# Attention in a three-layer kernel: the third bank of transposed scores is written later and alternates with the third score bank of the unit ahead

## The reference

```python
Q = x @ W_Q.T; K = x @ W_K.T; V = x @ W_V.T          # 16 heads of 8 features
attn = jnp.einsum('bhqd,bhkd->bhqk', Q, K) * scale
attn = jnp.where(causal, attn, -inf)
probs = jax.nn.softmax(attn, axis=-1)
y = jnp.einsum('bhqk,bhkd->bhqd', probs, V)
return y.transpose(0, 2, 1, 3).reshape(Bx, Sx, Dm) @ W_O.T
```

## Time and profile before

| | |
|---|---|
| median of 3 runs | 1352.4 us (1349.47 to 1357.5) |
| profiled execution | 1349.75 us, span 1348.0 us |
| TensorE (PE) busy, whole span | 1238.0 us (92%), 11940 products |
| VectorE busy | 1107.1 us (82%) |
| ScalarE busy | 833.5 us (62%) |
| GpSimd busy | 554.5 us (41%) |
| attention's turns, 430 to 958 us | PE 482.57, DVE 427.02, ACT 361.95, POOL 173.56 us busy; mean granted clock 0.97 |

### The profile page before, as it was taken

One profiled execution on the slowest core, in us unless ns is written; L12 is line 12 of the kernel. 1 busy time (PEld: TensorE's weight loads), 2 busy tenths in 40 slices (PEclk: granted clock), 3 DMA queues, 4 the chain that ended last, 5 costly groups with the idle time before them and its releaser, 6 DMA issues. The chain is left out here.

```text
span 1348.0 us, 34907 instructions
## 1 busy us (share of the span) xinstructions
PE 1238.0 (92%) x11940; PEld 691.8 (51%) x11940; DVE 1107.1 (82%) x2686; ACT 833.5 (62%) x1477; POOL 554.5 (41%) x658
## 2 busy tenths in 40 slices
PE   5999999999979999999999999899899999999998
PEld 2555555555533555555555555555455555555554
DVE  6888888888975688888888888888688898988876
ACT  5665565656543566666666666666565656566564
POOL 3454544544530233333333333333354554554444
PEclk9999999999995799999999999999899999999999
DMA  6000000000000000000000000000000000000000
GB/s 186 2 1 1 0 0 0 0 0 0 1 1 1 1 1 2 2 2 2 2 2 2 1 2 2 1 2 2 2 2 16 9 16 8 16 8 16 8 9 25
DMA packets 21417, 11.85 MB, mean 9 GB/s; under 512 B 960, under 2 KB 21312, under 8 KB 21312
## 3 DMA queue, kind: packets, MB, share of 16 engines
q1 hardware_dynamic: 21312, 10.43, 2.8%
HBM read 6.23 MB, written 4.19 MB: 8 GB/s over the span
## 5 line engine op out<-in xcount | busy, mean ns | idle before, releaser
L672 POOL TENSOR_TENSOR h_lo<-h,h_hi 128x512 f16<-128x512 f32 x288 | 337.7, 1173 | 386.3 <-ACT h_hi L634 375.6
L1109 DVE TENSOR_REDUCE neg_max_at<-score_at 128x2 f16<-128x512 f32 (+1 forms) x384 | 254.4, 692 | 78.1 <-PE score_at L940 72.5
L1229 POOL TENSOR_SCALAR_AFFINE_SELECT probs_at<-probs_at 128x512 f32<-128x512 f32 x256 | 157.0, 637 | 352.4 <-ACT probs_at L1187 351.9
L634 ACT ACTIVATE h_hi<-h 128x512 f16<-128x512 f32 x288 | 180.6, 627 | 152.7 <-DVE h L435 150.8
L1187 ACT ACTIVATE probs_at<-prob_at 128x512 f32<-128x512 f32 x384 | 201.6, 598 | 79.3 <-PE prob_at L972 77.4
L435 DVE TENSOR_TENSOR h<-prod,gate_b 128x512 f32<-128x512 f32 x256 | 174.9, 683 | 53.9 <-PE gate_b L543 53.7
L564 PE MATMUL y_b<-w_hi,h_hi 128*128 128x128 f16 x1152 | 207.8, 219 | 2.6 <-POOL h_lo L672 2.6
L564 PE MATMUL y_b<-w_hi,h_lo 128*128 128x128 f16 x1152 | 207.8, 219 | 0.0
L564 PE MATMUL y_b<-w_lo,h_hi 128*128 128x128 f16 x1152 | 207.8, 219 | 0.0
L429 DVE TENSOR_TENSOR prod<-silu,b 128x512 f32<-128x512 f32 x256 | 175.5, 686 | 37.9 <-ACT silu L623 23.6
L623 ACT ACTIVATE silu<-a 128x512 f32<-128x512 f32 x288 | 169.7, 589 | 49.7 <-PE a L530 48.3
(11 more groups left out here) (138 smaller groups left out, 2203.4 us busy)
## 6 DMA issues: line engine op xcount, KB each, us to landing
x<-in_L_attn_x_dram SPq DMA_DIRECT2D x16, 256.0 KB, 3.0
out_dram<-x SPq DMA_DIRECT2D x16, 256.0 KB, 2.3
raw_w<-in_L_ffn_w_dram SPq DMA_DIRECT2D x3, 512.0 KB, 5.2
raw_w<-in_L_ffn_sw_dram SPq DMA_DIRECT2D x3, 64.0 KB, 4.1
raw_attn<-in_L_attn_W_Q_dram SPq DMA_DIRECT2D x1, 64.0 KB, 4.9
raw_attn<-in_L_attn_W_K_dram SPq DMA_DIRECT2D x1, 64.0 KB, 3.6
raw_attn<-in_L_attn_W_V_dram SPq DMA_DIRECT2D x1, 64.0 KB, 3.6
raw_attn<-in_L_attn_W_O_dram SPq DMA_DIRECT2D x1, 64.0 KB, 3.7
```

Of the source, the lines that this page charges most:

```text
L634: nc.scalar.activation(h_hi[k][:, :], h[k][:, :], ACT.Copy).then_inc(hhi_done, 1)
L672: nc.gpsimd.tensor_tensor(h_lo[k][:, :], h[k][:, :], h_hi[k][:, :], ALU.subtract).then_inc(hlo_done, 1)
L1109: nc.vector.tensor_reduce(dst, src, AX.X, ALU.max, negate=True).then_inc(max_done, 1)
L1229: nc.gpsimd.affine_select(out=p, in_=p, compare_op=ALU.is_ge, fill=0.0, base=0, pattern=[[0, GROUPS], [1, P]], channel_multiplier=-1).then ...
```

## The change

The third transposed bank leaves `both`. A new `both_third` stands where score part 2 of the unit ahead stood, behind the jobs of the first place and `weigh`, and writes both, alternating: one score product of 256 keys, two transposed products of 128 queries, twice. Where there is no unit ahead (the last five units of the last turn), the third transposed bank alone is moved to the same place. The lists of ScalarE, VectorE and GpSimd and all waits stay as they are.

```diff
@@ -995,7 +995,16 @@
                         head_t(slot, b, j, i, h)
                         for k in range(beside * h, beside * (h + 1)):
                             score_head(later_slot, later_b, later_j, i, parts[i], k)
-                scores_t(c, slot, b, j, parts=(2,))
+
+            def both_third(c, slot, b, j, ahead):
+
+                later, later_slot, later_b, later_j = ahead
+                part = begin_scores(later, later_b, later_j, 2)
+                begin_t(c, b, j, 2)
+                for h in range(2):
+                    score_head(later_slot, later_b, later_j, 2, part, h)
+                    for k in range(2 * h, 2 * h + 2):
+                        head_t(slot, b, j, 2, k)
@@ -1022,7 +1031,7 @@
                         if ahead:
                             both(c, slot, b, j, ahead)
                         else:
-                            scores_t(c, slot, b, j)
+                            scores_t(c, slot, b, j, parts=(0, 1))
                         turn_jobs(job, c, slot, places[0])
@@ -1031,7 +1040,9 @@
                         if ahead:
-                            scores(*ahead, parts=(2,))
+                            both_third(c, slot, b, j, ahead)
+                        else:
+                            scores_t(c, slot, b, j, parts=(2,))
                         turn_jobs(job, c, slot, places[1])
```

## The result

The changed kernel took 1378.39, 1381.69, 1388.51 and 3800.25 us in four executions, a median of 1385.1; the fourth was disturbed and has no part in the ratio, and the other three alone have a median of 1381.69. The kernel before took 1350.93 in the runs beside them. The ratio is 1.0234, 95% interval 1.016 to 1.0308: the change makes the kernel slower, by about 2%. The profiled execution took 1378.39 us with a span of 1376.6, 28.6 more than the span before.

A forecast was written before the change was run, and what follows sets the result against it. No one engine bounds a turn; the path runs through TensorE, ScalarE or VectorE by unit. 16 turns at 1.26 (20.2 us) plus clock 2.4 on the profiled 1349.75 give 1372.3; forecast 1373, range 1354 to 1390.

The forecast's parts named there:

- forecast (d): The main forecast: each turn 1.26 us longer, two more clock falls, about 1373 us in all; chance 0.64.
- rival (c): Granted clock falls in most turns: ten to 14 falls of 1.2 us over the 20.2, giving 1382 to 1387; chance 0.16.
- Which engine holds what: Within a turn no single engine is the bound: TensorE is on the path in units 2, 4, 5, elsewhere ScalarE or VectorE.
- The group takes 0.32 and the drain stays: On TensorE, score and transposed products overlap fully, 0.32 us, saving 0.22 a unit; the 0.10 tiling change is still paid.
- the other end of the range: No overlap in the new TensorE group: it takes 0.22 us more and saves nothing, 0.88 more a turn, 14 us.
- Unit 3 begins 0.79 late: In unit 2 the late third Exp makes K00's copy 0.89 us late, so TensorE starts unit 3 0.79 late.
- VectorE's chain of fixed length from unit 3 to 4: Between units 3 and 4 VectorE sets the pace with fixed length, so the 0.79 us delay stays.
- Units 4 and 5 give back 0.22 each: TensorE bounds these units, so each returns the saved 0.22 us, leaving a delay of 0.35 at unit 6.
- y0's copy 1.26 late, the turn 1.26 longer: In unit 6 ScalarE's y0 copy is 1.26 us late; VectorE's yt_lo and x follow, so the turn grows 1.26.
- GpSimd's masks stay hidden: Before weighing, the second mask ends 1.81 us after the group's start, within TensorE's 1.92 of other work: 0.1 to spare.
- The clock: two more falls, 2.4 us: TensorE's longer pause before unit 3 and a second before v: 0 to 14 more falls possible, two taken, 2.4 us.
- The first turn: Of the 16 turns, the first and last miss some jobs but are priced alike, at 1.26 us more each.

## Why the prediction was right, and where it was off

The sign, the range (1354 to 1390; measured 1385.1, or 1381.69 without the disturbed execution) and the mechanism of the longer turn held. The clock did not go as the forecast (d) had it: by the prediction's own sign, a granted clock of 0.5 in many turns, the outcome is rival (c). By its own steps:

- **Which engine holds what.** Right. Sparing units 2 and 6 turned the loss of 1.40 a turn into a gain of 0.39; each alone cost 0.84 and 0.96.
- **The group takes 0.32 and the drain stays.** Right: 690.00 - 689.67 = 0.33 in unit 2. Its reason was incomplete, and the other end of the range was empty: the overlap doesn't come from alternating. Without it the turn is 0.05 longer, not 0.88.
- **Unit 3 begins 0.79 late.** Measured 0.87 ((692.75 - 677.79) against (684.17 - 670.08)). The third Exp starts 0.1 later than worked out, 12.35 behind the mark against 12.26. The one pause of about 1.8 us before unit 3 came as two, 1.06 before K01 and 0.92 before the masks: the wait for K00's bank is in the prediction's working, but not in its list of signs.
- **VectorE's chain of fixed length from unit 3 to 4.** Right: TensorE's masks of unit 4 stand where they should, and their wait for the maximum has grown from 0.33 to 0.49 us, since TensorE is 0.2 earlier and VectorE isn't.
- **Units 4 and 5 give back 0.22 each.** Right: the version with these two alone runs turns of 32.90, 0.43 less. In the changed kernel VectorE's maxima of unit 6 are 0.45 late ((705.24 - 677.79) against (697.08 - 670.08)), which is 0.87 less about twice 0.22.
- **y0's copy 1.26 late, the turn 1.26 longer.** Measured 1.40 for both (707.98 - 677.79 = 30.19 against 698.87 - 670.08 = 28.79).
- **GpSimd's masks stay hidden.** Right in the 14 turns: no weighing there shows a wait for them in the timeline. In the last turn, where no unit is ahead, weighing waits three times, 0.36, 1.44 and 1.04 us, where it waited once before, 1.75; that is part of the 2.9 lost behind the last mark.
- **The clock: two more falls, 2.4 us.** This term was mis-sized. There were nine lengthened turns, and against the turn's own length the clock cost 14.0 us in the profiled execution where 1.6 had been lost before: 12.4, not 2.4. Rival (c), with ten to 14 falls, had the size nearly right, though I gave it 0.16. I priced the falls by how often one had come behind a single pause of 1.0, while the change made two of it. That filling the pauses takes the falls away is shown; which turns are hit is not explained. With unit 2 alone moved, the same two pauses brought falls in the first three turns and none in the eleven after, with units 2 and 6 in nearly every turn.
- **The first turn.** Priced like the others at +1.26; it was 6.4 us shorter, because the clock rose earlier (435 us and a first mark at 462.5, against 457 and 468.9; two further traces have 447 and 465.8, 465 and 473.2). The other versions show it anywhere from 462.1 to 477.5 at the first mark, so it is no property of the change that I could show.
- **The sum.** Of the profiled execution it came near by luck. Predicted were 20.2 + 2.4 = 22.6 us more, measured 28.6: 19.6 for 14 turns, 12.4 for the clock, 2.9 at the end, and 6.4 less in the first turn. The 10.0 that the clock term lacked were in good part offset by the first turn. The other two undisturbed executions took 3 and 10 us longer at a lower mean granted clock (0.963 and 0.955 against 0.968); no trace divides them.

## What to carry to other kernels

When one engine's list is changed, walk the lists of its consumers: an instruction that now waits longer holds everything behind it there, and the remedy may be one line in the consumer's list, not in the producer's. Price a move by place: the same edit gave 0.22 in two units, nothing in four and cost 0.8 to 1.0 in two, so apply it where it pays. And look at the clock where an engine pauses: in one trace a gain of 0.43 a turn, 6 us in all, was lost whole to falls of the clock, and four unused products in one pause of the kernel before brought about as much (0.9947, 7 us, interval 3 to 12).

## What the runs showed of the hardware

TensorE started products out of the order in which the kernel issues them when they used another row group: in a list of two score products and four transposed ones the third started 0.11 us before the second, and in a list of four and two the fifth 0.01 us behind the first.

The Trainium skill (TensorE: Matmul & The Clock Gate, Part 3) says that matmuls start and end strictly in order, and that it is weight loads which are pulled ahead. These two traces disagree for the starts (476.35 ahead of 476.46, 749.51 ahead of 749.57); they say nothing of the ends.

The granted clock fell to 0.50 behind pauses as short as 1.0 us, alone (one of 14 turns before) or in pairs (nine of 14 after), though TensorE was at work for most of the time around them; with 0.86 us of products in each pause no fall was left in 14 turns.
